# A graph network kernel: edge rows gathered seven groups ahead, with a small fill of GpSimd's behind each gather

## What is computed

```python
h = jnp.maximum(_layernorm(x), 0.0)
# first layer, per edge and then per node
e = jnp.concatenate([h[src], edge_attr_16], axis=1)       # 200000 x 48
e = jnp.maximum(e @ w1a + b1a, 0.0) @ w1b + b1b           # 200000 x 96
s = jax.ops.segment_sum(e, dst, num_segments=12500)
agg = s / jnp.maximum(cnt, 1.0)[:, None]
x = x + (jnp.maximum(jnp.concatenate([h, agg], axis=1) @ w2a + b2a, 0.0) @ w2b + b2b)
# second layer: ten steps over all edges
f = jnp.maximum(_layernorm(x), 0.0)
for _ in range(10):
    f = 0.9 * (segment_sum((f * src_norm)[src], dst) * dst_norm) + 0.1 * feat0
x = x + f
```

## Time and profile before

| what | us |
|---|---|
| median of three runs | 6457.97 (6457.31 to 6459.14) |
| the profiled execution | 6459.22 |
| its span | 6457.6 |
| TensorE matmuls, busy | 5325.7 (82%) |
| VectorE, busy | 4263.8 (66%) |
| GpSimd, busy | 1699.1 (26%) |
| ScalarE, busy | 713.3 (11%) |

### The profile page before, as it was taken

The page is one execution under the profiler, slowest core; times in us unless marked ns, Lnnn a source line. Parts: engine busy times, 40 slices in busy tenths (PEclk is TensorE's granted clock), DMA queues, the critical chain, the costliest instruction groups (busy, mean ns, idle before and its releaser), DMA issues. The chain is left out here.

```text
span 6457.6 us, 211463 instructions
## 1 busy us (share of the span) xinstructions
PE 5325.7 (82%) x85008; PEld 3440.5 (53%) x85008; DVE 4263.8 (66%) x12554; ACT 713.3 (11%) x1731; POOL 1699.1 (26%) x1738
## 2 busy tenths in 40 slices
PE   1555556556556568999999999999999999999998
PEld 1445545545445454645656456565655656556454
DVE  7777777777777766666666666666666666666665
ACT  0233333333333200000000000000000000000000
POOL 2577777777777660000000000000000000000000
PEclk9877777777777778999999999999999999999999
DMA  4333333333333315555555555555555555555555
GB/s 113 107 96 96 95 99 92 96 94 94 98 95 96 93 30 194 186 206 188 204 196 196 198 195 197 205 185 200 193 206 196 193 198 195 193 207 188 202 190 171
DMA packets 442564, 1013.52 MB, mean 157 GB/s; under 512 B 253146, under 2 KB 371898, under 8 KB 387322
## 3 DMA queue, kind: packets, MB, share of 16 engines
q1 hardware_dynamic: 386938, 968.76, 42.8%
q0 software_dynamic: 54912, 33.89, 2.9%
HBM read 838.71 MB, written 176.58 MB: 157 GB/s over the span
## 5 line engine op out<-in xcount | busy, mean ns | idle before, releaser
L1697 PE MATMUL banks_fast<-count_units_fast,feature_parts_fast 128*32 128x512 fp8e3 x70608 | 3824.6, 379 | 47.1 <-DVE count_units_fast L1592 46.7
L1697 PEld LDWEIGHTS banks_fast<-count_units_fast,feature_parts_fast 128*32 128x32 bf16 x70608 | 2149.9, 97 | 1698.6 <-issue 51.9
L1591 DVE TENSOR_SCALAR count_units_fast<-packed_ring_fast 128x512 int32<-128x512 int32 x2949 | 1255.8, 426 | 1423.5 <-PE banks_fast L1697 1389.4
L139 POOL DMA_INDIRECT rows_fast<-row_table,idx_fast x1536 | 1497.1, 975 | 483.7 <-issue 451.4
L1592 DVE TENSOR_SCALAR count_units_fast<-packed_ring_fast 128x512 int32<-128x512 int32 x2949 | 1237.3, 420 | 0.0
L1106 DVE TENSOR_SCALAR window_place_hot_fast<-iota_wide_fast,local_keys_fast,target_weight_fast 128x196 bf16<-128x196 f16 x3136 | 947.5, 346 | 0.0
L1239 PE MATMUL banks_fast<-identity_fast,rows_fast 128*128 128x128 f32 x784 | 203.9, 352 | 714.4 <-DMA rows_fast<-row_table,idx_fast 711.3
L1222 PE MATMUL banks_fast<-window_place_hot_fast,window_src_hot_fast 128*128 128x196 bf16 x3136 | 608.5, 280 | 1.2 <-DVE window_place_hot_fast L1106 1.1
L1102 DVE TENSOR_TENSOR window_src_hot_fast<-iota_by_windows_fast,window_keys_fast 128x1024 bf16<-128x1024 bf16 x392 | 270.9, 691 | 485.9 <-PE banks_fast L1228 474.5
L1228 PE MATMUL banks_fast<-window_place_hot_fast,window_src_hot_fast 128*128 128x196 bf16 x3136 | 585.6, 273 | 0.0
L1239 PEld LDWEIGHTS banks_fast<-identity_fast,rows_fast 128*128 128x128 f32 x784 | 111.5, 179 | 732.1 <-DMA rows_fast<-row_table,idx_fast 407.8
(11 more groups left out here) (278 smaller groups left out, 1430.5 us busy)
## 6 DMA issues: line engine op xcount, KB each, us to landing
packed_ring_fast<-edge_counts SPq DMA_DIRECT2D x422, 1792.0 KB, 7.4
edge_counts<-count_stage_fast SPq DMA_DIRECT2D x100, 784.0 KB, 3.8
running_sums<-run_sums_fast SPq DMA_DIRECT2D x100, 768.0 KB
rows_fast<-row_table,idx_fast POOLq DMA_INDIRECT x1536
rows_fast<-attrs_padded SPq DMA_DIRECT2D x98, 128.0 KB, 4.0
attrs_padded<-in_edge_attr SPq DMA_DIRECT2D x1, 12500.0 KB, 41.4
row_table<-h_nodes_fast SPq DMA_DIRECT2D x1, 1568.0 KB, 14.7
edge_keys<-keys_fast SPq DMA_DIRECT2D x1, 1568.0 KB, 5.1
```

The source lines that it names most:

```text
L139: pool.indirect_dma_start(out=self.rows[:, s, c, 0:DN], out_offset=None, in_=b.dram.table, in_offset=bass.IndirectOffsetOnAxis(ap=idx[:, c ...
L1591: nc.vector.tensor_scalar(to[..., 0:P // 8], of, NIBBLES, None, ALU.bitwise_and)
L1697: last = nc.tensor.matmul(b.banks[at:at + DN, SWEEP[m % 2], 0:COLS], parts[:, side, j, k * DN:(k + 1) * DN], of_strip.bitcast(FP8), start= ...
```

## The change

Everything stays in the same kernel with the same arithmetic. Five things are done:

1. The buffers of gathered rows, their semaphores and their indices become a ring of seven groups (AHEAD_GROUPS) in place of two slots, and so do the edge keys. The loops of all engines hold 14 groups a turn (BATCH), and attributes are loaded five groups ahead.
2. Groups 0 to 6 are gathered before the loop, straight from the edge ends: three in `sorted_degrees`, one in `prepare_sorted`, three at the start of `messages_and_counts`. The loop gathers groups 7 to 97.
3. `setup` becomes `begin_loads` on this path: it only starts the loads, x first, and doesn't wait for them. `layer_norm_relu` waits for x alone. The split of the edge ends moves to the start of `sorted_degrees`, and the store of the table and the copy of the attributes are issued there by SyncE.
4. GpSimd's wait for `count_read` between the halves of a group goes. Behind each gather of the loop stands a memset of a 128x128 tile `pause`, and GpSimd waits for that memset.
5. VectorE copies a group's indices in the middle of the group seven before it, not at the start of the group one before.

```diff
+AHEAD_GROUPS = 7
+BATCH = 2 * AHEAD_GROUPS
+STARTED, HALFWAY = 3, 4
-        self.rows = ctx.enter_context(nc.sbuf_tensor(f"rows_{tag}", [P, SLOTS, G, 64], FP32))
+        self.rows = ctx.enter_context(nc.sbuf_tensor(f"rows_{tag}", [P, AHEAD_GROUPS, G, 64], FP32))
+    def gather_first(self, pool, b, edges, groups):
+
+        for r in groups:
+            self.gather(pool, b, r, edges.src[:, r * G:(r + 1) * G], range(G))
...
+def begin_loads(nc, b, edges, ins, loads):
...
+        @block.sync
+        def _(sp):
+            x = ins["x"]
+            sp.dma_start(per_node(b.x[:, :])[:, 0:J - 1, :], x[0:P * (J - 1), :].rearrange("(j p) d -> p j d", p=P)).then_inc(loads.x_in, 16)
+            sp.wait_ge(x_filled, 1)
...
+            if x_in is not None:
+                dve.wait_ge(x_in, 32)
...
-            for s in range(SLOTS):
-                ahead.gather(pool, b, s, edges.src[:, s * G:(s + 1) * G], range(G))
+            pool.wait_ge(stored, 16)
+            pool.wait_ge(split, 6)
+            ahead.gather_first(pool, b, edges, range(0, STARTED))
...
+            ahead.gather_first(pool, b, edges, range(STARTED, HALFWAY))
...
-            with pool.Fori(1, n_loops) as i:
-                for s in range(SLOTS):
-                    g = i * SLOTS + s
-                    pool.wait_ge(turned, (g + 1) * Q)
+            def step(i, t):
+
+                g, k, r = i * BATCH + t, i * PAIRS_A_LOOP + t // SLOTS, t % AHEAD_GROUPS
+                pool.wait_ge(turned, (SLOTS + g + 1) * Q)
...
+                pool.wait_ge(indexed, g + 1)
+                pool.sem_inc(taken, 1)
+                for c in range(G):
+                    ahead.gather(pool, b, r, idx[:, r, :], range(c, c + 1))
+                    nc.gpsimd.memset(pause[:, :], 0.0).then_inc(paused, 1)
+                    pool.wait_ge(paused, g * G + c + 1)
                     pool.sem_inc(taken, 1)
-                    ahead.gather(pool, b, s, idx[:, s, :], range(G // 2))
-                    pool.wait_ge(count_read, (g + 1) * READS + READS // Q)
-                    pool.sem_inc(taken, 1)
-                    ahead.gather(pool, b, s, idx[:, s, :], range(G // 2, G))
+
+            ahead.gather_first(pool, b, edges, range(HALFWAY, HALFWAY + 1))
+            pool.wait_ge(keys_pointed, 1)
+            for r in range(KEYS_AHEAD):
+                fetch_keys(r)
+            ahead.gather_first(pool, b, edges, range(HALFWAY + 1, AHEAD_GROUPS))
+            with pool.Fori(0, n_loops - 1) as i:
+                for t in range(BATCH):
+                    step(i, t)
+            for t in range(BATCH - AHEAD_GROUPS):
+                step(n_loops - 1, t)
...
-                    nc.vector.tensor_copy(idx[:, 1 - s, :], edges.src[:, bass.ds((g + 1) * G, G)]).then_inc(indexed, 1)
...
+                        if q == Q // 2:
+                            nc.vector.tensor_copy(idx[:, r, :], edges.src[:, bass.ds((g + AHEAD_GROUPS) * G, G)]).then_inc(indexed, 1)
```

More of the change, by code:

```diff
@@ L396, in step, with split_ends @@
                 dve.wait_ge(made, n[0])
+            def split_ends(ends, part, place, before):
+                nc.vector.tensor_scalar(low[:, :], ends, P - 1, None, ALU.bitwise_and).then_inc(split, 1)
+                nc.vector.tensor_scalar(high[:, :], ends, BITS, None, ALU.logical_shift_right).then_inc(split, 1)
+                dve.wait_ge(split, before + 2)
+                nc.vector.tensor_copy(part[:, :], low[:, :]).then_inc(split, 1)
+                nc.vector.tensor_copy(place[:, :], high[:, :]).then_inc(split, 1)
+                dve.wait_ge(split, before + 4)
+            nc.vector.memset(zero_rows[:, :], 0.0).then_inc(split, 1)
+            dve.wait_ge(loads.ends_in, 6 * 16)
+            split_ends(edges.src[:, 0:T], edges.src_part, edges.src_place, 1)
+            nc.vector.scalar_tensor_tensor(out=edges.src[:, 0:T], in0=edges.src_part[:, :], scalar=float(J), in1=edges.src_place[:, :],
+                                           op0=ALU.mult, op1=ALU.add).then_inc(split, 1)
+            split_ends(edges.dst[:, :], edges.dst_part, edges.dst_place, 6)
             first = node[:, 0:1]
@@ L716, in start_again @@
         def start_again():
-            nc.gpsimd.sem_clear(range(low, high + 1))
+            for counter in counters:
+                nc.gpsimd.sem_clear(range(counter.num, counter.num + 1))
             nc.all_engine_barrier()
@@ L779, in _, with prepare_sorted @@
             sp.wait_ge(stored, 32)
-def prepare_sorted(nc, b, edges, ins, kept):
+def prepare_sorted(nc, b, edges, ins, kept, ahead):
     same, cont, last_row, window_row, unsorted, overfull = kept
@@ L1016, in store_sums, with load_attrs, step @@
                              sums[:, s, :, :]).then_inc(sums_out[s], 16)
[L1018 to L1020 removed]
+            def load_attrs(g, r):
+                sp.dma_start(rows[:, r, :, DN:DI], attrs[:, bass.ds(g * G, G) if not isinstance(g, int) else slice(g * G, (g + 1) * G), :]) \
+                    .then_inc(attrs_in[r], 16)
+            def step(i, t):
+                g, s = i * BATCH + t, t % SLOTS
+                if not isinstance(g, int) or g + ATTRS_AHEAD < J:
                     sp.wait_ge(turned, (g + 1) * Q)
                     sp.sem_inc(passed, 1)
[L1023 to L1031 removed]
+                    load_attrs(g + ATTRS_AHEAD, (t + ATTRS_AHEAD) % AHEAD_GROUPS)
+                sp.wait_ge(count_read, (g + 1) * READS)
+                sp.sem_inc(passed, 1)
+                store_counts(s, g)
+                sp.wait_ge(summed, g * RUN_STEPS + 1)
+                sp.sem_inc(passed, 1)
+                store_sums(s, g)
+            for g in range(ATTRS_AHEAD):
+                load_attrs(g, g)
+            with sp.Fori(0, n_loops - 1) as i:
+                for t in range(BATCH):
+                    step(i, t)
+            for t in range(BATCH):
+                step(n_loops - 1, t)
             for s in range(SLOTS):
@@ L1152, in _ @@
                 act.sem_inc(passed, 1)
-                for s in range(SLOTS):
-                    g = i * SLOTS + s
+                for t in range(BATCH):
+                    g, k, s = i * BATCH + t, i * PAIRS_A_LOOP + t // SLOTS, t % SLOTS
                     def read_counts(u):
```

201 lines of the change are left out of this document (123 added, 78 removed).

## The result

The changed kernel took 7509.72 us (median of four runs, 7508.29 to 7510.45); the kernel before, run beside it, 6457.64 (6456.22 to 6459.14). The ratio is 1.163, with an interval of 1.161 to 1.164: 1052 us slower. The forecast was 7500.

A forecast was written before the change was run, and what follows sets the result against it. GpSimd's back-to-back gathers were taken as the bound: loop from 228 us, 58 for key gathers, 1456 row gathers at 2.05 us, ending at 3271, 1040 later; 6459 + 1040 = 7500 us, own range 7165 to 7820, 8-in-10 range 6800 to 7800.

The forecast's parts named there:

- The bound: Row-gathering phase: it ends when GpSimd has issued its last gather, at 3271 us, 1040 later than before.
- The loop's start: GpSimd enters its loop near 228 us with groups 0 to 6 gathered; the early start is worth 83 us.
- The pitch: p, time from one gather to the next in GpSimd's loop: 2.05 us, bounds 1.82 and 2.27.
- The 0.13 us between a gather and the fill: From a gather's end to the memset behind it: 0.13 us, taken as belonging to the gather's end, bounds 0 and 0.30.
- The gap after the release: From the memset's release to the next gather, with an increment between: 0.74 us, bounds 0.68 and 0.79.
- the two rows with the same form: Two earlier trace rows, VectorE's copy end to GpSimd's gather with an increment between: 0.79 us both times.
- The subtraction of 0.11 for a release of oneself: GpSimd releasing itself: 0.17 us, 0.11 less than 0.28, which made 0.68 the gap's lower bound.
- 45 key gathers: Key gathers in GpSimd's loop, counted at 58 us in all.
- TensorE's wait for rows: TensorE's waits for gathered rows rise from 711 to about 1790 us.
- The wait exposes only the semaphore: Rival on GpSimd's held gather: release costs 0.28 us, 1.585 us from gather to gather, time 6820 us; chance 0.12.
- The fill is free: Rival: fill and wait fit the 0.30 us between gathers, 1.279 us each, time 6376 us; chance 0.08.
- The waits vanish: Rival: gathering ahead removes TensorE's 711 us of waits, VectorE sets 15.1 us a group, time about 5915; chance 0.02.

The follow-up runs named there:

- half_before: Kernel before without its wait for count reads, 8 of 16 columns of a group gathered in the loop: 6600.3 us, on the chip where the kernel before took 7280.
- before_long_loop: Kernel before without its wait for count reads, TensorE's loop written for 14 groups a turn: 7672.4 us against 7279.5, ratio 1.054.

## Why the prediction was right, point by point

**The bound.** GpSimd's pace sets the end of the phase, before and after. In the changed kernel GpSimd's last gather ends at 3273.2 (forecast 3271), and from there to the end of the span it is 4235.2 us, against 4226.7 before. The end of GpSimd's loop moved by 1042 us, and what lies behind it became 8.5 us longer. The 8.5 were not in the sum ("nothing after this phase changes"); the ten steps alone grew by 10.3.

**The loop's start.** Forecast 228, measured 227.23. The steps to it were looser: the stage ahead ended at 18.4 as said, the normalisation ran 19.0 to 40.9, but the table's store had landed 5.2 us after its start and not 14.7 (the forecast's 0.36 + 14.3). The copy of the attributes ran beside it before (from 32.56 us, for 41 us) and starts at 48.54 now, behind it; that this is the cause was not tested. The first gather was thus at 49.12 and not at 56, held by the split of the edge ends. The 7 us were lost again: the next stage started at 125.3 and not 129, the one after at 158.0 and not 159. VectorE set the last of these, as forecast: GpSimd's gathers of that stage were done at 155.7. The forecast of 228 was thus closer than its steps.

**The pitch.** Forecast 0.975 + 0.13 + 0.20 + 0.74 = 2.05, measured 0.981 + 0 + 0.225 + 0.810 = 2.016 as a mean, 1.96 in the plain case. Two terms were mis-sized:

- The 0.13 us between a gather and the fill are not there (1503.35 + 0.95 = 1504.30). I had put the difference between 0.30 and 0.17 to the gather's end. It stands ahead of a gather that follows a gather, as the version with one wait shows, and the fill takes it away. That was the lower bound.
- The gap after the release is 0.79 and not 0.74 (0.810 as a mean, with the groups' ends that have no key gather in it). The halfway value was a hedge; the two rows with the same form had both said 0.79, and they held to 0.01. The subtraction of 0.11 for a release of oneself does not apply: with the wait on the gather GpSimd's own release took 0.27, as VectorE's did (0.28).

**The groups' ends** were what the sum had missed. I had counted 1.28 us for each of 45 key gathers, 58 us. They took 3046.0 - 2936.1 = 110 us, 2.44 each, because the gap ahead of each is 1.58 in most of them: what the sequencer has to do at a group's end is exposed by the held wait just ahead of it. The argument was in the prediction ("exposes what the sequencer otherwise does under the previous gather"), but it was applied to one increment only. So 52 us too few here and 1456 x 2.05 - 2936.1 = 49 too many in the pitch; that 3271 came so close to 3273 is luck to that extent. The mechanism, a held wait with an increment between it and the gather, was right.

**TensorE's wait for rows**: forecast 1790, measured 1741.

**The rivals.** *The wait exposes only the semaphore* is what happens without the increment, at 6776 us (its estimate was 6820). The prediction's "by that page p would be this rival's" asked more of the Trainium skill than its section says: that section has the wait on the gather, and the changed kernel has it ahead of an increment. *The fill is free* needed a pitch under 1.336; a fill whose wait comes once a group reaches 1.34, and with its ends of groups it takes 6658 us. With no fill at all it is 6389, 13 us over the 6376 that the rival gave: 11 of them lie behind the last gather, nearly all in the ten steps. *The waits vanish* did not come by gathering ahead (598 us remained), only by halving the gathers.

## What to carry to other kernels

Look at what stands between a wait that really holds an engine's sequencer and the instruction that is to follow it. Here one increment between them cost 0.5 us a gather, and several waits and increments 1.2 us at a group's end, while behind a wait that was met long ago the same instructions cost nothing. Let the instruction carry the wait itself where that can be done. In this kernel, where the bounding engine runs back to back, deeper buffers added nothing, and only an earlier start or less of its work did; ask of a "late" transfer whether its issuer ever rested. And the longer loop bodies were not free for another stage (10 us in 3940): compare a stage whose code did not change, too.

## What the runs showed of the hardware that was not expected

A 128x128 memset on GpSimd takes 0.22 us and starts at once behind an indirect DMA; a 128x1 one still takes 0.11. The indirect DMA starts 0.17 us behind it and 0.30 us behind another indirect DMA, so a fill between two of them costs 0.09 us net.

One of the chips ran the loop over the groups much slower, with the ten steps unharmed: the kernel before took 7280 us there and 6455 to 6463 elsewhere, the ring with half of its gathers 6574 and 5924. The ten steps took the same as elsewhere (3942.7 us in `half_before`, 3938.9 to 3942.0 elsewhere for the short loops). The timeline of `before_long_loop` shows what its groups look like:

```profile
1503.48 0.37 ACT L1164 COPY turn_fast<-banks_fast 128x256 f32<-128x256 f32 x1 [2.09 <-remote]
...
1507.74 0.53 PE L1226 MATMUL banks_fast<-window_place_hot_fast,window_src_hot_fast 128*128 128x196 bf16 x2
...
1521.89 0.69 DVE L1099 TENSOR_TENSOR window_src_hot_fast<-iota_by_windows_fast,window_keys_fast 128x1024 bf16<-128x1024 bf16 x1 [13.25 <-remote]
1521.94 0.50 ACT L1159 CAST count_stage_fast<-banks_fast 128x392 uint16<-128x392 f32 x1 [18.09 <-remote]
```

TensorE's matmuls on record end at 1508.3, and VectorE and ScalarE, which take up their work after counts of TensorE's, both go on only at 1521.9, within 0.05 us of each other. Both rows name `remote` as what released them, which is a release that the profile puts down to no recorded instruction; some of TensorE's records can be missing. What held the two for 13 us, no view says. GpSimd's gathers run on at 1.25 us through it. It stays open.
